# Layer 0 of a two-layer FFT convolution: the upper half of a row's base bank moves into the next row's mix

## The chip, the cores and the metric

The kernel runs on one core of one Trainium2 chip. The metric is the device time of one execution in microseconds (us). Five engines work side by side, each through its own instructions in order: TensorE (PE; its weight loads are listed apart as PEld), VectorE (DVE), ScalarE (ACT), GpSimd (POOL) and SyncE (SP, which here issues most DMAs). They meet at semaphores only.

## The reference, cut to what matters

```
# x: (8, 16, 512, 512) f32; w_real, w_imag: (16, 16, 3, 3); b_real, b_imag: (16,)
X  = rfftn(gn(x), axes=(-2, -1))                       # gn: group norm, 8 groups
Yr = conv3x3(Xr, wr) - conv3x3(Xi, wi) + b_real        # on the spectrum
Yi = conv3x3(Xr, wi) + conv3x3(Xi, wr) + b_imag
x  = x + irfftn(Yr + 1j * Yi)                          # layer 0
x  = x + mean_filter_15x15(gn(x))                      # layer 1
```

A 3x3 convolution of the spectrum is, in the image, a product with cosines and sines of the row and column number. So layer 0 needs no transform: per image row it mixes the 16 channels with a matrix that depends on the row, multiplies three such mixtures by 1, a cosine and a sine along the row, and adds them. As only half of the spectrum is convolved, each mixture takes the row itself (g) and its Hilbert transform along the row (h), a fixed 512-wide convolution.

## The kernel before, in words

The eight images run one after the other; first layer 0, then layer 1. A partition holds one channel and one block of 64 rows (16 channels x 8 blocks = 128 partitions), so a step over t = 0..63 handles eight rows of every channel at once; "a row" below is such a step. Each f32 operand is split into a high and a low f16 part, and each product is made of three f16 products.

Per row n of layer 0:

- **ACT** normalises the row (L750 into the high part of gp, L753 into g32). **POOL** subtracts for the low part (L1291, `split_g`).
- **PE** transposes it (L442, 8 matmuls, `front_turn`); **ACT** copies the transpose to SBUF (L759); **PE** does the Hilbert product (L452, 12 matmuls, `front_hilbert`) into `h_ps`; **ACT** keeps its high part (L767) and **DVE** the low part (L1096, `low_hilbert`, signal `h_split`).
- **PE** mixes (`mix`, L556 and L570). The array is used as four 64x64 tiles. "Lower" matmuls read partitions 0 to 63, "upper" ones 64 to 127; each half-term is one matmul to either half of the output. There are three PSUM banks to fill: the base p0 (in a ring of four banks), and p1 and p2, of which there is one each. Each bank takes three lower and three upper half-terms, p0 also two wrap terms. A mix has ten steps r = 0..9, each with a lower and an upper part (4 matmuls of 64x512), that write different banks. Since both parts add to the same bank at different steps, the second one waits for a semaphore of the first (`p1_half`, `p0_half`, `p2_half`).
- **DVE** multiplies p1 and p2 by the waves (L1138, L1144, `wave_terms`, signals `t1_done`, `t2_done`); **POOL** adds the two (L1298) and adds the image row (L1300, signal `q_done`); **DVE** adds p0 and writes the row (L1153) and takes its statistics (L1156): `finish_row`. Later **DVE** makes a correction per parity (L1163, `half_mean`), which **ACT** adds to the row (L775, `add_half_row`). For rows 1 to 6 and 57 to 63 **POOL** also sums rows for layer 1 (L1311, L1314, `presum`): in slots 6 to 12 and at the end.
- **SP** fetches the row's matrices from DRAM, 192 KB and 32 KB, into a ring of four (`fetch`), as soon as `p0_ready` tells that the old ones are read.

The order of all this is written out by hand. In slot n PE does `front_hilbert(n+1)`, `front_turn(n+2)`, `mix(n)`; ACT `normalise(n+3)`, `keep_hilbert(n+1)`, `keep_turned(n+2)`, `add_half_row(n-4)`; DVE `wave_terms(n-1)`, `half_mean(n-3)`, `low_hilbert(n+1)`, `finish_row(n-2)`; POOL `split_g(n+3)`, `add_terms(n-1)`. NG = 4 rows are written out and looped over (`Fori`), the first and last rows stand outside the loop. The gp buffers are a ring of NG, the hp buffers (high and low part of h) a ring of two.

## Time and profile before

| | |
|---|---|
| three runs | 4042.79 us (median), 4030.65 and 4044.06 us |
| profiled execution | 4036.1 us, its span 4034.3 us |
| granted TensorE clock, mean | 0.962 |
| busy share of PE, DVE, ACT, POOL | 90%, 81%, 59%, 65% |
| layer 0 of one image | some 305 us of a period of some 482 us |

The times are in us from the start of the span; a matmul's duration in the trace runs to the end of its drain, so consecutive matmuls overlap, and the distance of two starts is what a step costs. "Idle before" counts gaps of an engine; "issue" is a gap for which the profile shows no releaser.

### The profile page before, as it was taken

The page shows a single profiled execution, that of the slowest core. Times are in us where ns is not written, and L with a number is a line of the kernel's source. Part 1 is how long each engine was busy: PE and PEld are TensorE (multiplying, and loading weights), DVE is VectorE, ACT ScalarE, POOL GpSimd, SP SyncE. Part 2 cuts the span into 40 slices and gives each one's busy share as a digit, 9 for nine tenths or more (in the row PEclk, how much of TensorE's full clock was granted, in tenths as well). Part 3 has the DMA queues.
Part 4 walks back from the last instruction along what each step waited for, and adds up shares of the span by engine and source line. Part 5 has one row for each costly group of instructions (what it writes and reads, how often), then busy time and mean ns, then how long its engine had stood idle before and what let it go on. Part 6 is the DMA issues. An engine that isn't in the chain of part 4 may idle for free.

```text
span 4034.3 us, 124977 instructions
## 1 busy us (share of the span) xinstructions
PE 3628.3 (90%) x42592; PEld 2549.3 (63%) x42592; DVE 3254.2 (81%) x6382; ACT 2386.4 (59%) x3774; POOL 2638.4 (65%) x2177
## 2 busy tenths in 40 slices
PE   3299989998999989999899997999899998999988
PEld 1166576665766667666676666666576665766667
DVE  7878877887778878788787887788877887879986
ACT  0078733886348852588427883288733886248852
POOL 5078853887539865488546885388853986638865
PEclk8599999999999999999999999999999999999999
DMA  7511156111751118311382114711165111741114
GB/s 162 168 44 52 42 170 180 51 52 32 217 145 50 52 47 244 101 52 52 94 237 61 52 50 134 213 46 52 39 191 162 53 52 34 228 129 51 52 50 137
DMA packets 228434, 406.73 MB, mean 101 GB/s; under 512 B 98160, under 2 KB 173520, under 8 KB 215888
## 3 DMA queue, kind: packets, MB, share of 16 engines
q1 hardware_dynamic: 205776, 285.88, 24.7%
q10 hardware_dynamic: 22400, 117.46, 10.9%
q8 instruction: 156, 2.56, 0.3%
q14 instruction: 102, 0.84, 0.1%
HBM read 256.31 MB, written 146.80 MB: 100 GB/s over the span
## 4 chain that ended last, share of the span: by engine, by line
PE 70%; POOL 9%; DVE 9%; issue 7%; ACT 3%; ACTq 1%; DMA 1%; SPq 1%; POOLq 0%; DVEq 0%
PE p L556 21%; PE h_ps L651 14%; PE h_ps L452 14%; PE p L677 6%; PE xt_ps L442 5%; PE p L490 4%; POOL ob_all L1298 3%; POOL arena L1291 2%; PE h_ps L556 2%; POOL ob_all L1300 2%; PE p L570 2%; DVE ob_all L1223 2%; ACT arena L720 1%; POOL arena L1314 1%; PE p L459 1%
## 5 line engine op out<-in xcount | busy, mean ns | idle before, releaser
L556 PE MATMUL p<-arena,bd_all 64*64 64x512 f16 x16896 | 1343.7, 381 | 19.6 <-issue 11.9
L1291 POOL TENSOR_TENSOR arena<-arena 128x512 f16<-128x512 f32 x512 | 593.6, 1159 | 518.8 <-ACT arena L753 499.3
L556 PEld LDWEIGHTS p<-arena,bd_all 64*64 64x64 f16 x16896 | 606.9, 105 | 450.5 <-issue 279.3
L1349 POOL TENSOR_TENSOR arena<-img 128x512 f32<-128x512 f32 x392 | 499.2, 1274 | 468.8 <-PE h_ps L651 443.4
L720 ACT ACTIVATE arena<-h_ps 128x512 f16<-128x512 f32 x512 | 305.6, 597 | 840.9 <-PE h_ps L651 596.5
L452 PE MATMUL h_ps<-hilbert,arena 128*128 128x256 f16 x6144 | 759.6, 273 | 0.0
L452 PEld LDWEIGHTS h_ps<-hilbert,arena 128*128 128x128 f16 x6144 | 560.4, 98 | 267.4 <-issue 195.0
L1300 POOL TENSOR_TENSOR ob_all<-ob_all,img 128x512 f32<-128x512 f32 x512 | 663.5, 1296 | 79.3 <-POOL ob_all L1298 66.8
L1298 POOL TENSOR_TENSOR ob_all<-ob_all 128x512 f32<-128x512 f32 x512 | 656.9, 1283 | 31.5 <-DVE ob_all L1144 30.5
L750 ACT ACTIVATE arena<-img,sc 128x512 f16 (+1 forms) x512 | 442.1, 864 | 327.9 <-PE p L570 215.0
L1096 DVE SCALAR_TENSOR_TENSOR arena<-h_ps,arena 128x512 f16<-128x512 f32 x512 | 353.1, 690 | 268.0 <-ACT arena L767 268.0
L759 ACT ACTIVATE arena<-xt_ps 128x1024 f16<-128x1024 f16 x512 | 518.7, 1013 | 35.2 <-PE xt_ps L442 35.2
L651 PE MATMUL h_ps<-bd_all,arena 128*128 128x128 f32 x3584 | 539.5, 286 | 0.0
L775 ACT ACTIVATE img<-img,half_row (+1 forms) x1024 | 488.8, 534 | 74.4 <-DVE half_row L1163 74.4
L651 PEld LDWEIGHTS h_ps<-bd_all,arena 128*128 128x128 f32 x3584 | 447.6, 191 | 121.2 <-issue 115.1
L1207 DVE TENSOR_TENSOR arena<-h_ps,arena 128x512 f16<-128x512 f32 x512 | 353.3, 690 | 206.5 <-ACT arena L720 205.1
L1138 DVE SCALAR_TENSOR_TENSOR ob_all<-p,bias_c,cosw 128x256 f32<-128x256 f32 x1024 | 442.1, 474 | 2.4 <-issue 2.0
L1144 DVE SCALAR_TENSOR_TENSOR ob_all<-p,bias_c,cosw 128x256 f32<-128x256 f32 x1024 | 444.0, 475 | 0.0
L753 ACT ACTIVATE arena<-img,sc 128x512 f32 (+1 forms) x512 | 433.6, 847 | 4.3 <-POOL arena L1291 4.3
L1156 DVE BATCH_NORM_STATS2 stat<-img (+1 forms) x512 | 355.6, 694 | 62.8
L677 PE MATMUL p<-band,arena 128*128 128x135 f16 (+1 forms) x4096 | 332.4, 224 | 61.7 <-DVE ob_all L1223 60.3
L490 PE MATMUL p<-img,bd_all 128*64 128x256 f32 x2048 | 310.9, 411 | 72.8 <-POOL bd_all L1270 47.0
(163 smaller groups left out, 4686.4 us busy)
## 6 DMA issues: line engine op xcount, KB each, us to landing
out<-ob_all SPq DMA_DIRECT2D x512, 256.0 KB, 4.1
bd_all<-bd_dram SPq DMA_DIRECT2D x512, 192.0 KB, 2.3
img<-in_x ACTq DMA_DIRECT2D x168, 512.0 KB, 7.1
img<-in_x ACTq DMA_DIRECT2D x112, 256.0 KB, 4.8
wrap_mat<-tab_wrap_h SPq DMA_DIRECT2D x512, 32.0 KB, 2.0
img<-in_x SPq DMA_DIRECT2D x24, 512.0 KB, 24.6
bd_dram<-ob_all SPq DMA_DIRECT2D x16, 768.0 KB, 3.5
img<-in_x SPq DMA_DIRECT2D x16, 256.0 KB, 7.3
```

The costliest lines, as they stand in the source:

```text
L452: m = mm(dst(a), xT[:, 4 * lx + k, 0:rows], tb["hilbert16"][:, lt, k, 0:cols], start=(half == 0 and i == 0), stop=(half == 1 and i == 2))
L490: m = mm(uv_ps[i * HP:(i + 1) * HP, cols], w, img[:, 2 * q + i, cols], start=(q == 0 and part == 0), stop=(q == T // 2 - 1 and part == 1), ...
L556: m = mm(bank[out_half * HP:(out_half + 1) * HP, :], low(half, 6 * lm + (j if own else j + 1)), (g_part if own else h_part)(half, lp), sta ...
L651: m = mm(turned_ps[u % 2][:, k, :], row[:, k * P:(k + 1) * P], mat, start=(i == 0), stop=(i == len(terms) - 1))
L677: m = mm(p0[0][:, lo:hi], parts[u % 2][:, l, k, :], tb["band16"][:, lo - k * P + R:hi - k * P + R], start=(u == 0 and k == 0 and l == 0), ...
L759: nc.scalar.activation(xT.rearrange("p k (s m) -> p k s m", s=2)[:, :, ::-1, :], xt_ps[:].rearrange("p k (s m) -> p k s m", s=2), ACT.Iden ...
L775: ins = nc.scalar.activation(row, row, ACT.Identity, bias=half_row[:, s, a:a + 1])
L1144: ins = V.scalar_tensor_tensor(t2[:, a, :], p2[:, a * HALF:(a + 1) * HALF], bias_c[:, 0, t, 1 - a:2 - a], sinw[:, a, :], ALU.add, ALU.mult)
L1291: G.tensor_tensor(gp[s][:, 1, :], g32, gp[s][:, 0, :], ALU.subtract).then_inc(g_split, 1)
L1298: G.tensor_tensor(q, term_row[s % 2][0], term_row[s % 2][1], ALU.add).then_inc(t_added, 1)
L1300: G.tensor_tensor(q, q, parity(img[:, t, :]), ALU.add).then_inc(q_done, 1)
L1349: G.tensor_tensor(diff[u % 2], img[:, u + R, :], img[:, u - R - 1, :], ALU.subtract).then_inc(moved, 1)
```

## The change: one part of the mix is put off by a row, rings get longer, one DVE operation changes place

What it does, part by part:

- `mix(n)` opens p1 (lower) and p2 (upper) first. The lower part then does p0(n) and its lower wrap term and ends with p2; the upper part does, in steps 3, 4, 8 and 9, what is left of the *previous* row's p0 (`late_base(n-1)`: its upper half-terms and upper wrap term, signal `p0_ready` for row n-1), and p1 in steps 5 to 7. The wait for `t2_done` moves to the front of the mix. After row 63 a `late_base` of its own closes the last base bank.
- NG becomes 8 for the gp ring and for the loop bodies; a new RB = 4 is the ring of p0, of the fetched matrices and of hp (before 2). The arena grows from 12 to 16 rows of 2 KB, and the scratch that the program keeps for DMA descriptors is set to 8192 bytes.
- In a DVE slot `finish_row(n-2)` stands ahead of `low_hilbert(n+1)`.

```diff
 NU = 3 * C
 NV = P
 QUARTER = HALF // 4
-NG = 4
+NG = 8
+RB = 4
 GROUP_T = 4
 REC = 12 * HP
...
+        arena = sb("arena", [P, 16 * W])
+        piece = [arena[:, i * W:(i + 1) * W] for i in range(16)]
         g32 = piece[0]
         gp = [piece[1 + s].bitcast(F16).rearrange("p (l j) -> p l j", l=2) for s in range(NG)]
-        uv32, uvT = piece[8], piece[9].rearrange("p (k m) -> p k m", k=4)
-        xT = piece[5].bitcast(F16).rearrange("p (k m) -> p k m", k=8)
-        hp = [piece[6 + s].bitcast(F16).rearrange("p (l a n) -> p l a n", l=2, a=2) for s in range(2)]
-        smat = arena[:].bitcast(F16).rearrange("p (t j o) -> p t j o", t=T, j=12)
+        uv32, uvT = piece[7], piece[8].rearrange("p (k m) -> p k m", k=4)
+        xT = piece[9].bitcast(F16).rearrange("p (k m) -> p k m", k=8)
+        hp = [piece[10 + s].bitcast(F16).rearrange("p (l a n) -> p l a n", l=2, a=2) for s in range(RB)]
+        smat = arena[:, 0:12 * W].bitcast(F16).rearrange("p (t j o) -> p t j o", t=T, j=12)
...
@@ -376,12 +377,12 @@
                     sp.dma_start(wrap_mat[s][:], tab["wrap_h16"][t]).then_inc(bd_in[s], 16)
 
                 sp.wait_ge(uv_summed, PRIMED + (b + 1) * NCH)
-                for t in range(NG):
+                for t in range(RB):
                     fetch(t, t)
-                with sp.Fori(1, T // NG) as i:
-                    for s in range(NG):
-                        sp.wait_ge(p0_ready, b * T + i * NG + (PRIMED + s - NG + 1))
-                        fetch(i * NG + s, s)
+                with sp.Fori(1, T // RB) as i:
+                    for s in range(RB):
+                        sp.wait_ge(p0_ready, b * T + i * RB + (PRIMED + s - RB + 1))
+                        fetch(i * RB + s, s)
 
             with sp.Fori(0, B - 1) as b:
@@ -537,56 +538,53 @@
                     if first * NG + s + 2 < T:
                         front_turn(n + 2, (s + 2) % NG)
 
-                def mix(i, s, first):
-                    n = b * T + i * NG + s
-
-                    def low(h, j):
-                        return bd[s][h * HP:(h + 1) * HP, j, :]
-
-                    def g_part(h, l):
-                        return gp[s][h * HP:(h + 1) * HP, l, :]
-
-                    def h_part(h, l):
-                        return hp[s % 2][h * HP:(h + 1) * HP, l]
+                def operands(s):
 
                     def half_terms(bank, j, i3, half, opens, closes):
                         lm, lp = ((0, 0), (0, 1), (1, 0))[i3]
+                        rows = slice(half * HP, (half + 1) * HP)
                         for own in (True, False):
                             out_half = half if own else 1 - half
+                            part = gp[s][rows, lp, :] if own else hp[s % RB][rows, lp]
                             m = mm(bank[out_half * HP:(out_half + 1) * HP, :],
-                                   low(half, 6 * lm + (j if own else j + 1)),
-                                   (g_part if own else h_part)(half, lp),
+                                   bd[s % RB][rows, 6 * lm + (j if own else j + 1), :], part,
                                    start=opens and i3 == 0, stop=closes and i3 == 2, skip_group_check=True)
                         return m
-                    pe.wait_ge(bd_in[s], 32 * (b * (T // NG) + i + 1))
-                    pe.wait_ge(h_split, PRIMED + n + 1)
-                    pe.wait_ge(t1_done, PRIMED + n)
-                    if first > 0:
-                        pe.wait_ge(x1_done, PRIMED + n - (NG - 1))
-                    pe.sem_inc(mix_step, 1)
 
                     def wrap_terms(half, closes):
                         for out_half in (half, 1 - half):
-                            m = mm(p0[s][out_half * HP:(out_half + 1) * HP, :],
-                                   wrap_mat[s][half * HP:(half + 1) * HP, out_half * HP:(out_half + 1) * HP],
+                            m = mm(p0[s % RB][out_half * HP:(out_half + 1) * HP, :],
+                                   wrap_mat[s % RB][half * HP:(half + 1) * HP, out_half * HP:(out_half + 1) * HP],
                                    wrap_row[half * HP:(half + 1) * HP, :], start=False, stop=closes,
                                    skip_group_check=True)
                         return m
+                    return half_terms, wrap_terms
+
+                def late_base(s, steps):
+
+                    half_terms, wrap_terms = operands(s)
+                    for i3 in steps:
+                        if i3 < 3:
+                            half_terms(p0[s % RB], 0, i3, 1, False, False)
+                        else:
+                            wrap_terms(1, True).then_inc(p0_ready, 1)
...
+                        elif r == 6:
                             if first == 0 and s == 0:
                                 pe.wait_ge(v_wrap, b + 1)
                                 pe.sem_inc(mix_step, 1)
                             wrap_terms(0, False).then_inc(p0_half, 1)
-                        elif r < 7:
-                            if r == 4:
-                                pe.wait_ge(p1_half, n + 1)
-                                pe.sem_inc(mix_step, 1)
-                            m = half_terms(p1[:], 2, r - 4, 0, False, True)
@@ -597,27 +595,33 @@
 
                     def upper(r):
                         if r < 3:
-                            m = half_terms(p1[:], 2, r, 1, True, False)
+                            m = half_terms(p2[:], 4, r, 1, True, False)
                             if r == 2:
-                                m.then_inc(p1_half, 1)
-                        elif r < 6:
-                            if r == 3:
-                                pe.wait_ge(t2_done, PRIMED + n)
+                                m.then_inc(p2_half, 1)
+                        elif r in (3, 4, 8, 9):
+                            if first * NG + s > 0:
+                                if r == 3:
+                                    pe.wait_ge(p0_half, n)
+                                    pe.sem_inc(mix_step, 1)
+                                late_base((s - 1) % NG, (r - 3,) if r < 5 else (r - 6,))
+                        else:
+                            if r == 5:
+                                pe.wait_ge(p1_half, n + 1)
                                 pe.sem_inc(mix_step, 1)
-                            m = half_terms(p2[:], 4, r - 3, 1, True, False)
-                            if r == 5:
-                                m.then_inc(p2_half, 1)
-                        elif r < 9:
-                            if r == 6:
-                                pe.wait_ge(p0_half, n + 1)
-                                pe.sem_inc(mix_step, 1)
-                            half_terms(p0[s], 0, r - 6, 1, False, False)
-                        else:
-                            wrap_terms(1, True).then_inc(p0_ready, 1)
-
+                            m = half_terms(p1[:], 2, r - 5, 1, False, True)
+                            if r == 7:
+                                m.then_inc(p1_ready, 1)
+
+                    pe.wait_ge(bd_in[s % RB], 32 * (b * (T // RB) + i * (NG // RB) + s // RB + 1))
+                    pe.wait_ge(h_split, PRIMED + n + 1)
+                    pe.wait_ge(t1_done, PRIMED + n)
+                    pe.wait_ge(t2_done, PRIMED + n)
+                    if first * NG + s >= RB:
+                        pe.wait_ge(x1_done, PRIMED + n - (RB - 1))
+                    pe.sem_inc(mix_step, 1)
                     for r in range(10):
-                        for part in ((upper, lower) if r in (4, 7) else (lower, upper)):
-                            part(r)
+                        lower(r)
+                        upper(r)
 
                 front(0, 0, 0)
...
@@ -640,6 +644,9 @@
                 for s in range(NG):
                     front(T // NG - 1, s, T // NG - 1)
                     mix(T // NG - 1, s, T // NG - 1)
+                pe.wait_ge(p0_half, (b + 1) * T)
+                pe.sem_inc(mix_step, 1)
+                late_base(NG - 1, range(4))
                 group_mean(b * 2 + 2)
                 group_variance(b * 2 + 2)
 
@@ -762,14 +769,15 @@
 
                 def keep_hilbert(n, s, first=1):
                     act.wait_ge(h_made, PRIMED + n + 1)
-                    if first * NG + s > 1:
-                        act.wait_ge(p0_ready, PRIMED + n - 1)
-                    nc.scalar.activation(hp[s % 2][:, 0], halves(h_ps[:, 0]), ACT.Identity,
+                    if first * NG + s >= RB:
+                        act.wait_ge(p0_ready, PRIMED + n - (RB - 1))
+                    nc.scalar.activation(hp[s % RB][:, 0], halves(h_ps[:, 0]), ACT.Identity,
                                          scale=1.0 / TAB_SCALE).then_inc(h_kept, 1)
...
                     if t + 2 < T:
                         keep_turned(n + 2)
                     if t >= 4:
-                        add_half_row(n - 4, i * NG + s - 4, s)
+                        add_half_row(n - 4, i * NG + s - 4, (s - 4) % NG)
 
                 for s in range(NG):
...
@@ -1170,10 +1178,10 @@
                         wave_terms(n - 1, i * NG + s - 1, (s - 1) % NG, first - (s < 1))
                     if t >= 3:
                         half_mean(n - 3, i * NG + s - 3, (s - 3) % NG, first - (s < 3))
+                    if t >= 2:
+                        finish_row(n - 2, i * NG + s - 2, (s - 2) % NG, first - (s < 2))
                     if t + 1 < T:
                         low_hilbert(n + 1, (s + 1) % NG)
-                    if t >= 2:
-                        finish_row(n - 2, i * NG + s - 2, (s - 2) % NG, first - (s < 2))
 
                 slot(0, 0, 0)
                 virtual_means()
@@ -1374,7 +1382,7 @@
     import concourse.bacc as bacc
     from concourse.bass_utils import run_bass_kernel_spmd
 
-    nc = bacc.Bacc("TRN2", target_bir_lowering=False, num_devices=1)
+    nc = bacc.Bacc("TRN2", target_bir_lowering=False, num_devices=1, dynamic_dma_scratch_size=8192)
     arrays, args = {}, []
```

On PE, the opening of a mix in the loop. `p0_0` and `h_ps` are banks of the p0 ring. Before:

```order
L565 REGISTER_ALU [waits t1_done]
L556 MATMUL p0_0<-arena,bd_all 64x512 [waits x1_done]
L556 MATMUL p0_0<-arena,bd_all 64x512
L556 MATMUL p1<-arena,bd_all 64x512 x2
L556 MATMUL p0_0<-arena,bd_all 64x512 x2
```

With the change:

```order
L549 MATMUL p1<-arena,bd_all 64x512 [waits t2_done,x1_done,t1_done,bd_in0,h_split]
L549 MATMUL p1<-arena,bd_all 64x512
L549 MATMUL p2<-arena,bd_all 64x512 x2
L549 MATMUL p1<-arena,bd_all 64x512 x2
L549 MATMUL p2<-arena,bd_all 64x512 x2
```

The first matmul now waits for `t2_done` too, and the banks p1 and p2 are opened in place of p0 and p1.

On PE, the middle of the same mix, from step 3 on. Before:

```order
L570 MATMUL p0_0<-wrap_row,wrap_mat0 64x512 x2
L556 MATMUL p2<-arena,bd_all 64x512 [waits t2_done]
L556 MATMUL p2<-arena,bd_all 64x512 x3
L556 MATMUL p1<-arena,bd_all 64x512 [waits p1_half]
L556 MATMUL p1<-arena,bd_all 64x512 x3
L556 MATMUL p2<-arena,bd_all 64x512 x2
L556 MATMUL p1<-arena,bd_all 64x512 x2
L556 MATMUL p0_0<-arena,bd_all 64x512 [waits p0_half]
L556 MATMUL p0_0<-arena,bd_all 64x512 x3
L556 MATMUL p2<-arena,bd_all 64x512 [waits p2_half]
L556 MATMUL p2<-arena,bd_all 64x512 x3
```

With the change (`p0_2` is the bank of the row before):

```order
L549 MATMUL p0_0<-arena,bd_all 64x512 x2
L549 MATMUL p0_2<-arena,bd_all 64x512 [waits p0_half]
L549 MATMUL p0_2<-arena,bd_all 64x512
L549 MATMUL p0_0<-arena,bd_all 64x512 x2
L549 MATMUL p0_2<-arena,bd_all 64x512 x2
L549 MATMUL p0_0<-arena,bd_all 64x512 x2
L549 MATMUL p1<-arena,bd_all 64x512 [waits p1_half]
L549 MATMUL p1<-arena,bd_all 64x512
L556 MATMUL p0_0<-wrap_row,wrap_mat0 64x512 x2
L549 MATMUL p1<-arena,bd_all 64x512 x2
L549 MATMUL p2<-arena,bd_all 64x512 [waits p2_half]
L549 MATMUL p2<-arena,bd_all 64x512
```

Each bank's second half now stands three steps (p1) and five steps (p2) behind its first half's last matmul, where it stood two and two steps behind before, counted from the step of the signal to the step of the wait; `p0_half` is that of the row before.

On DVE, one slot of the loop. Before:

```order
L1163 SCALAR_TENSOR_TENSOR half_row<-stat,known 128x2
L1095 REGISTER_ALU
L1096 SCALAR_TENSOR_TENSOR arena<-h_ps,arena 128x512 [waits h_kept]
L1153 ISA [waits p0_ready,q_done]
L1153 SCALAR_TENSOR_TENSOR img<-p0_2,sc,ob_all 128x2x256
L1156 ISA [waits x1_done]
L1156 BN_STATS stat<-img 128x6
```

With the change:

```order
L1171 SCALAR_TENSOR_TENSOR half_row<-stat,known 128x2
L1161 ISA [waits p0_ready,q_done]
L1161 SCALAR_TENSOR_TENSOR img<-p0_1,sc,ob_all 128x2x256
L1164 ISA [waits x1_done]
L1164 BN_STATS stat<-img 128x6
L1103 REGISTER_ALU
L1104 SCALAR_TENSOR_TENSOR arena<-h_ps,arena 128x512 [waits h_kept]
```

The two operations of `finish_row` have passed the low half of h.

## Rows read from the trace of the kernel before

**Rows 1.** The page's head: span, then busy time and share of each engine.
```profile
span 4034.3 us, 124977 instructions
...
PE 3628.3 (90%) x42592; PEld 2549.3 (63%) x42592; DVE 3254.2 (81%) x6382; ACT 2386.4 (59%) x3774; POOL 2638.4 (65%) x2177
```
**Rows 2.** Busy time in 20 rows' stretch of layer 0: PE, PEld, DVE, ACT, POOL, clock.
```profile
314.00:402.40 88.40, 88.40 (x1202) 57.17 (x1201) 73.88 (x161) 77.22 (x121) 73.98 (x61) 1.00 0.19 52
```
**Rows 3.** Who waited for whom in that stretch: us, times, longest.
```profile
DVE arena L1096 <- ACT arena L767: 11.7, 20, 0.6
POOL arena L1291 <- ACT arena L753: 10.6, 20, 0.6
PEld p L556 <- issue: 10.1, 40, 0.3
ACT arena L750 <- PE p L570: 8.4, 15, 0.6
...
ACT arena L750 <- PE h_ps L570: 3.4, 6, 0.6
```
**Rows 4.** Timeline, one row on PE and PEld: start, us, what, count [idle before].
```profile
350.14 0.84 PE L556 MATMUL p<-arena,bd_all 64*64 64x512 f16 x12
350.59 0.11 PEld L570 LDWEIGHTS p<-wrap_row,wrap_mat 64*64 64x64 f16 x2
350.81 0.38 PE L570 MATMUL p<-wrap_row,wrap_mat 64*64 64x512 f16 x2
351.11 0.46 PEld L556 LDWEIGHTS p<-arena,bd_all 64*64 64x64 f16 x12 [0.18 <-issue]
351.14 0.80 PE L556 MATMUL p<-arena,bd_all 64*64 64x512 f16 x9
351.90 0.17 PEld L556 LDWEIGHTS p<-arena,bd_all 64*64 64x64 f16 x6 [0.32 <-issue]
352.36 0.41 PE L556 MATMUL p<-arena,bd_all 64*64 64x512 f16 x2
352.69 1.48 PE L452 MATMUL h_ps<-hilbert,arena 128*128 128x256 f16 x12
354.01 0.61 PE L442 MATMUL xt_ps<-ident,arena 128*128 128x128 f16 x8
354.56 0.84 PE L556 MATMUL p<-arena,bd_all 64*64 64x512 f16 x12
```
**Rows 5.** Timeline, the other engines over the same row.
```profile
352.83 0.86 DVE L1138 SCALAR_TENSOR_TENSOR ob_all<-p,bias_c,cosw 128x256 f32<-128x256 f32 x2
353.61 0.86 DVE L1144 SCALAR_TENSOR_TENSOR ob_all<-p,bias_c,cosw 128x256 f32<-128x256 f32 x2
354.39 0.15 DVE L1163 SCALAR_TENSOR_TENSOR half_row<-stat,known 128x2 f32 x1
354.54 0.57 ACT L767 ACTIVATE arena<-h_ps 128x512 f16<-128x512 f32 x1
355.15 0.69 DVE L1096 SCALAR_TENSOR_TENSOR arena<-h_ps,arena 128x512 f16<-128x512 f32 x1 [0.61 <-ACT arena L767]
355.76 0.74 DVE L1153 SCALAR_TENSOR_TENSOR img<-h_ps,sc,ob_all 128x512 f32 x1
356.64 0.69 DVE L1156 BATCH_NORM_STATS2 stat<-img  x1
```
**Rows 6.** Timeline of POOL, first and last of seven presums, and rows between.
```profile
246.26 1.28 POOL L1311 TENSOR_TENSOR arena<-img 128x512 f32<-128x512 f32 x1
...
267.36 1.15 POOL L1291 TENSOR_TENSOR arena<-arena 128x512 f16<-128x512 f32 x1
272.30 1.16 POOL L1291 TENSOR_TENSOR arena<-arena 128x512 f16<-128x512 f32 x1
276.03 1.28 POOL L1314 TENSOR_TENSOR arena<-arena,img 128x512 f32<-128x512 f32 x1
```
**Rows 7.** Timeline of PE there: the Hilbert products of following rows.
```profile
262.61 1.48 PE L452 MATMUL h_ps<-hilbert,arena 128*128 128x256 f16 x12
267.02 1.48 PE L452 MATMUL h_ps<-hilbert,arena 128*128 128x256 f16 x12
271.73 1.48 PE L452 MATMUL h_ps<-hilbert,arena 128*128 128x256 f16 x12
276.66 1.48 PE L452 MATMUL h_ps<-hilbert,arena 128*128 128x256 f16 x12
281.62 1.49 PE L452 MATMUL h_ps<-hilbert,arena 128*128 128x256 f16 x12
286.41 1.48 PE L452 MATMUL h_ps<-hilbert,arena 128*128 128x256 f16 x12
```
**Rows 8.** The chain at the end of an image: ACT's branch to the next image.
```profile
1152.39 4.36 issue
1156.75 0.06 ACTq L877
```
**Rows 9.** The page's DMA issues of the fetched matrices: KB, us to landing.
```profile
bd_all<-bd_dram SPq DMA_DIRECT2D x512, 192.0 KB, 2.3
...
wrap_mat<-tab_wrap_h SPq DMA_DIRECT2D x512, 32.0 KB, 2.0
```

**Rows 10.** Timeline at the end of an image's layer 0: last mix, last row.
```profile
497.12 0.41 PE L556 MATMUL p<-arena,bd_all 64*64 64x512 f16 x2
...
502.14 0.75 DVE L1153 SCALAR_TENSOR_TENSOR img<-p,sc,ob_all 128x512 f32<-128x512 f32 x1 [1.22 <-POOL ob_all L1300]
```

35 lines of the change are left out of this document (19 added, 16 removed).

## The prediction, made before the kernel was run

> **What bounds the kernel now.** I read the page's head first [rows 1]: PE is busy 90% of the span, DVE 81%. Such shares are an average over two layers, so next came the table of stretches for 20 rows in the middle of layer 0 [rows 2]. There PE is busy for all of 88.40 us, at a granted clock of 1.00, which is the higher of its two levels (2.4 GHz); a row costs 88.4 / 20 = 4.42 us. DVE is busy 73.88 / 20 = 3.69 us a row, ACT 77.22 / 20 = 3.86, POOL 73.98 / 20 = 3.70. The waits of that stretch [rows 3] say the same from the other side: DVE, ACT and POOL each stand idle some 0.5 to 0.6 us per row, and PE's matmuls never do. So PE sets the row, and a wait of the other three is worth nothing by itself. But "busy" counts a matmul to the end of its drain, and hides what PE loses between starts. What gives it away is the line of PEld: 40 gaps in 20 rows, 10.1 us in all, two a row, before weights of the mix.
>
> The timeline of one row shows them [rows 4]. The mix opens at 350.14, step 2 starts at 350.59, step 3 at 350.81: the first step costs 0.24 us, each further one 0.215. At that pace step 4 would follow at 351.025; but the lower part, which waits for p1_half there, starts at 351.14: 0.115 lost. Three steps on, step 7 should start at 351.785; its weights, held by p2_half, come at 351.90, and a matmul starts 0.03 after its weights (as 351.11 and 351.14): 351.93, so 0.145 lost. From there to the last step is 2 x 0.215 again (352.36). Sum 0.26 us a row; both are the time that a signal takes from a matmul's start to the start of the one that waits: 350.59 to 351.14 is 0.55, and for p2_half 351.355 to 351.93 is 0.57. The mix takes 2.55, the Hilbert product 1.32, the transposes 0.55.
>
> **The change part by part.**
>
> *The order of the mix.* Matmuls and weight loads stay the same in number. p1_half now has three steps between signal and wait, 0.645 against the 0.55 to 0.57 needed; p2_half five; p0_half is a row old. Both stalls go, with 0.08 to spare for the tighter one. As the two parts no longer run apart (0.03 at the end of the mix) I take 0.27 a row: 4.42 becomes 4.15. Bounds: one of the two signals still late would leave 0.12 of it; more than 0.30 isn't there to be gained, as ten steps, the Hilbert product and the transposes stay.
>
> *The wait for t2_done in front of the mix.* Behind it stand all matmuls of the mix, and behind these all of DVE's next row. In the trace t2 of the row before ends at 353.61 + 0.86 = 354.47 and the mix opens at 354.56 [rows 4, 5]: with DVE's old phase this wait would decide at once. But that phase is late without need: DVE idles 0.61 before L1096 [rows 3, 5], where it waits for ACT, and the row's end stands behind it. In the new order the end of the row comes first and fills that hole. p1 is complete with step 7, whose matmuls start 0.24 + 6 x 0.215 = 1.53 after the opening; with 0.55 for the signal DVE can start L1138 at 2.08; L1138 and L1144 take 354.47 - 352.83 = 1.64, so t2 is done at 3.72, and a signal of at most 0.2 later is 3.92, under 4.15. DVE's own round is 4.42 - 0.61 = 3.81 and fits as well. Cost nothing, with 0.2 to 0.3 of cover.
>
> *Low half of h behind the row's end.* It ends a round of 3.81 after L1138's start, 5.89 after the opening. The Hilbert product that needs it starts one row and one mix later, 4.15 + (2.55 - 0.27) = 6.43. Cost nothing, 0.5 of cover. This cover is gone where POOL delays the end of a row, as DVE then stands before L1153 with the low half behind it.
>
> *Rings.* The gp ring of eight takes away ACT's wait for the mix (L750, 8.4 + 3.4 = 11.8 us of 20 rows [rows 3]), hp's ring of four one that isn't seen. ACT isn't the bound: worth nothing, bounds 0 and 0.1 a row. p0_ready comes a row later, so SP fetches a row later: it has two rows, 8.3 us, where 2.3 and 2.0 us are needed [rows 9]. Nothing.
>
> *The presums.* Here it costs. With a presum POOL needs 272.30 - 267.36 = 4.94 a row [rows 6], seven rows long (246.26 to 276.03). Before, POOL falls behind by 7 x (4.94 - 4.42) = 3.6 us, of which PE lost: its rows last 4.71, 4.93, 4.96 and 4.79 in place of 4.42 [rows 7], 1.7 us. With rows of 4.15 POOL falls behind by 7 x 0.79 = 5.5. Before, 1.9 were absorbed; now the way over the row's end and the low half has only the 0.5 found above, so I take 5.0 (bounds 3.6 and 5.5). That is 3.3 more than before (1.9 to 3.8).
>
> *Start and end of an image.* After row 63 PE has four steps more, some 0.9 us. PE's last matmul starts at 497.12, the last row is finished at 502.14, held by POOL [rows 10]: hidden. The first two rows wait for other things; 0, between -0.5 and +0.5.
>
> *Sum.* 60 of the 63 rows behind the first have a Hilbert product ahead and gain: 60 x 0.27 = 16.2. Less 3.3: 12.9 us an image, 103 for eight. Layer 1 keeps its instructions. The profiled execution took 4036.1 us (span 4034.3), so 3933. The three runs' mean is 3 us above the profiled one, their median 7; I give 3936.
>
> **The rivals.**
>
> *A wait on another engine eats part of it.* Covers of 0.08 (p1_half), 0.2 (t2_done) and 0.3 (ACT's 3.86 against 4.15, DVE's 3.81) are thin, and all of them are sized at the old phases. For it: three engines come within 0.3 of PE. Against it: none of their rounds exceeds 4.15. If half a stall (0.13) comes back, 60 x 8 x 0.13 = 62 us: 3998.
>
> *It gains more.* If POOL's delay in the presums is absorbed as before, and the mixes lose their last 0.03: 4036 - 8 x (60 x 0.30 - 1.9) = 3907.
>
> *The stalls only change place.* If t2_done keeps the phase of the trace, the opening comes at 354.47 + 0.14 = 354.61, later than now, and the round through DVE and the mix would hold at about 4.42: 4036, no change. Against it: the 0.61 of idle time in front of L1096 is there to be used.
>
> *The longer loop bodies miss their instructions: slower.* The inner loops now have 8 rows written out in place of 4. In the trace a jump back costs nothing there: the rows from 262.61 to 267.02, or from 350.14 to 354.56, are all 4.42. But at the jump to the next image, over a long body, ACT stands for 4.36 us [rows 8]. If a body of 8 rows is too long for an engine's store of instructions, each of 5 jumps in 8 images costs that: 40 x 4.36 = 174, less 103 gained: 4107. It decides from 103 / 40 = 2.6 us a jump on. The Trainium skill ("Runtime: NRT & Kernel Launch", Instruction fetch mechanics) says that a taken branch to a page outside the window forces a fetch before execution goes on; 4.36 us of standing at the long jump agree. It gives PE 128 KiB and the others 32, and in the same section a window of two lines of 16 KiB. PE runs 120 matmuls and loads a row [rows 2]; at the page's 64 bytes each, eight rows are an estimated 61 KB, inside the first figure and outside the second, as four rows (31 KB) barely are inside. ACT, DVE and POOL, with 6, 8 and 3 operations a row [rows 2], have bodies far shorter than that. By the second figure PE would jump to a page that is gone, by the first not.
>
> **How the numbers follow.** The forecast 0.62, with a range of its own from 3918 to 3958 (0.03 a row is 14 us, the presums' bounds 11 and 4, the start 4, the runs' spread 7). Part eaten 0.16, more gained 0.07, stalls moved 0.06, slower 0.09. A measurement of this kernel tells 0.3% (12 us) from no change; so faster 0.85, same 0.06, slower 0.09. The range for 8 in 10 takes in the forecast and most of the part-eaten case: 3905 to 3995.
>
> **What would show it.** Right: rows of 4.15 us in the middle of layer 0 with PE still busy throughout and no PEld gap of 0.18 and 0.32 inside the mix; L1104 (low half) behind L1164 with no idle time before it; ACT's wait for L556 (the wrap matmul) gone; five or six rows of 4.94 around the presums in each image, with PE's wait on DVE or POOL there. Wrong: a gap before each mix's first weights released by L1152 (t2_done); rows of 4.3; a stall of some us once in eight rows on PE (the jump); or a period of alternating rows, which would mean a ring of waits through two engines that this sum treats one by one.

## The result, and the profile after

The changed kernel took 4029.48 us (median of 20 runs, 4024.04 to 4033.87) against 4037.36 (20 runs, 4029.03 to 4044.44) for the kernel before: ratio 0.9978, 95% interval 0.9972 to 0.9984. That is 8 us, inside the 0.3% called no change, where 3936 was forecast.

In the tables below a row of layer 0 is the time from one row's Hilbert product to the next, and "an image's rows" is the time from its first to its last, read at the first image: 280.5 us before, 280.4 after. The other images lie within 0.5 us of the first, but for the last one of the profile before, which took 284.6. So the rows did not change in sum, though they were to lose 12.9 us.

The page's head after, the span, the busy time of each engine and what the final chain ran over:
```profile
span 4028.9 us, 122552 instructions
...
PE 3515.2 (87%) x42592; PEld 2538.7 (63%) x42592; DVE 3445.0 (86%) x6382; ACT 2382.8 (59%) x3774; POOL 2638.3 (65%) x2177
...
PE h_ps L658 14%; PE p L549 11%; PE h_ps L453 9%; PE p L684 6%; PE p L491 4%; POOL ob_all L1306 3%; DVE arena L1104 3%; DVE ob_all L1152 3%; DVE half_row L1171 3%; PE xt_ps L443 3%; DVE img L1161 2%; POOL ob_all L1308 2%; POOL arena L1299 2%; DVE ob_all L1231 2%; ACT arena L727 1%
```
The same stretch as in [rows 2], after (PE, PEld, DVE, ACT, POOL, clock), and the waits in it, which answer to [rows 3]:
```profile
314.00:402.40 88.40, 83.83 (x1204) 56.95 (x1200) 85.55 (x161) 76.65 (x121) 73.66 (x61) 1.00 0.19 51
```
```profile
PEld h_ps L453 <- issue: 12.3, 17, 0.9
ACT arena L774 <- PE h_ps L453: 12.1, 21, 0.8
POOL arena L1299 <- ACT arena L760: 11.7, 21, 0.8
PE h_ps L453 <- DVE arena L1104: 4.3, 10, 0.5
```
Read these against [rows 1 to 3]. PE is no longer busy throughout: 4.6 of 88.4 us are idle, and it stands in front of the Hilbert product for DVE's low half, in one row of two. ACT's wait for the wrap matmul and PEld's 40 gaps inside the mix are gone, as the change intends. DVE has the same 161 instructions in the stretch as before but 85.55 us of work in place of 73.88: 11.7 us, 0.58 a row, that no instruction was added for. The page says 3445.0 for 3254.2 over the whole span. A count that stays and a busy time that grows is the line to stop at: some instruction takes longer.

It is the half mean, a SCALAR_TENSOR_TENSOR on two elements a partition. Below, an instruction is said to stand while it is on its engine, counted as busy, and does not finish because another engine's instruction has not. DVE's timeline over two rows after (answers to [rows 5]):
```profile
353.35 0.64 DVE L1171 SCALAR_TENSOR_TENSOR half_row<-stat,known 128x2 f32 x1
353.91 0.74 DVE L1161 SCALAR_TENSOR_TENSOR img<-h_ps,sc,ob_all 128x512 f32 x1
354.79 0.69 DVE L1164 BATCH_NORM_STATS2 stat<-img  x1
355.40 0.67 DVE L1104 SCALAR_TENSOR_TENSOR arena<-h_ps,arena 128x512 f16<-128x512 f32 x1
356.04 0.88 DVE L1146 SCALAR_TENSOR_TENSOR ob_all<-p,bias_c,cosw 128x256 f32<-128x256 f32 x2
356.83 0.87 DVE L1152 SCALAR_TENSOR_TENSOR ob_all<-p,bias_c,cosw 128x256 f32<-128x256 f32 x2
357.62 0.99 DVE L1171 SCALAR_TENSOR_TENSOR half_row<-stat,known 128x2 f32 x1
...
360.03 0.67 DVE L1104 SCALAR_TENSOR_TENSOR arena<-h_ps,arena 128x512 f16<-128x512 f32 x1
```
and POOL's over the same time:
```profile
352.81 1.16 POOL L1299 TENSOR_TENSOR arena<-arena 128x512 f16<-128x512 f32 x1 [0.34 <-ACT arena L760]
...
357.44 1.16 POOL L1299 TENSOR_TENSOR arena<-arena 128x512 f16<-128x512 f32 x1 [0.74 <-ACT arena L760]
...
361.65 1.16 POOL L1299 TENSOR_TENSOR arena<-arena 128x512 f16<-128x512 f32 x1 [0.34 <-ACT arena L760]
```
The half mean took 0.15 in [rows 5]; here 0.64 and 0.99. It ends at 353.99 and 358.61; POOL's low part of g ends at 353.97 and 358.60. The longer it takes, the earlier it began in POOL's instruction; the end is always POOL's end. Over the whole span it took 144.2 us before (median 151 ns, 116 of 512 over 250 ns) and 360.7 after (median 690, 416 over 250, longest 1220), and each long one ends 14 to 16 ns (median; at most 21) after a tensor_tensor of POOL. The converse holds too: of the 512 half means, those that began outside a POOL instruction, or with less than 0.15 us of it left, all took at most 168 ns (386 before, 90 after). Of two that begin together the half mean can be the one that goes first: in five rows after, the half mean began at most 0.04 us behind the start of POOL's low part of g and took 0.15, and POOL's instruction took 1.19 to 1.22 in place of 1.16 (the first at 236.25). Of the other lines of DVE's row none got longer. In the row of [rows 5] it began at 354.39, between one POOL instruction that ended at 354.19 and the next that began at 354.71.

The hint was in the profile of before. The table of groups, with forms kept apart, has (busy, mean ns):
```profile
L1163 DVE SCALAR_TENSOR_TENSOR half_row<-stat,known 128x2 f32 x416 | 106.4, 256 | 0.0
L1163 DVE SCALAR_TENSOR_TENSOR half_row<-stat,known 128x2 f32<-128x2 f32 x96 | 37.2, 394 | 0.0
```
A mean of 256 and 394 ns for an instruction whose row in the timeline reads 0.15 says that it has two durations. It also sets right what stands ahead of the prediction, that the engines "meet at semaphores only": here two of them meet in an instruction that waits for no semaphore.

**Why just 4.42 us again.** After the presums the rows alternate, 4.13 to 4.29 and 4.58 to 4.73, mean 4.42. The same rows close a ring over two rows. The half mean ends with POOL's instruction at 353.97; the row's end, the statistics and the low half follow, to 356.07 (2.10); PE's Hilbert product starts at 356.14 (0.07); then PE and ACT:
```profile
356.14 1.48 PE L453 MATMUL h_ps<-hilbert,arena 128*128 128x256 f16 x12
```
```profile
357.74 0.60 ACT L774 ACTIVATE arena<-h_ps 128x512 f16<-128x512 f32 x1 [0.38 <-PE h_ps L453]
358.23 1.02 ACT L766 ACTIVATE arena<-xt_ps 128x1024 f16<-128x1024 f16 x1
359.14 0.95 ACT L783 ACTIVATE img<-img,half_row  x2
359.99 0.84 ACT L757 ACTIVATE arena<-img,sc 128x512 f16 x1
360.72 0.86 ACT L760 ACTIVATE arena<-img,sc 128x512 f32 x1
```
ACT's high half starts 1.60 after the Hilbert product, its queue is through with g at 361.58 (3.84), POOL's low part of g starts at 361.65 and ends at 362.81 (1.23), and the half mean of that row, begun at 362.19, ends at 362.83. 2.10 + 0.07 + 1.60 + 3.84 + 1.23 = 8.84 us for two rows, 4.42 each. The other row of the pair has a ring of its own (358.60 to 367.44, again 8.84). The old bound was PE's 4.42, the new one a ring through DVE, PE, ACT and POOL that has the same length by chance: the experiments below move the one without the other.

### The profile page after: what moved, and what is told of

The parts are those of the page before. It is cut to its first block, busy times and chain, and to the rows that moved or that the text cites. A ratio compares the mean times of both kernels' runs of the same rounds, so it can differ in the third digit from the quotient of the medians.

```text
span 4028.9 us, 122552 instructions
## 1 busy us (share of the span) xinstructions
PE 3515.2 (87%) x42592; PEld 2538.7 (63%) x42592; DVE 3445.0 (86%) x6382; ACT 2382.8 (59%) x3774; POOL 2638.3 (65%) x2177
## 3 DMA queue, kind: packets, MB, share of 16 engines
q14 instruction: 150, 1.23, 0.1%
## 4 chain that ended last, share of the span: by engine, by line
PE 52%; DVE 21%; issue 11%; POOL 8%; ACT 5%; ACTq 1%; DVEq 1%; SPq 1%; DMA 0%; POOLq 0%
PE h_ps L658 14%; PE p L549 11%; PE h_ps L453 9%; PE p L684 6%; PE p L491 4%; POOL ob_all L1306 3%; DVE arena L1104 3%; DVE ob_all L1152 3%; DVE half_row L1171 3%; PE xt_ps L443 3%; DVE img L1161 2%; POOL ob_all L1308 2%; POOL arena L1299 2%; DVE ob_all L1231 2%; ACT arena L727 1%
## 5 line engine op out<-in xcount | busy, mean ns | idle before, releaser
L549 PE MATMUL p<-arena,bd_all 64*64 64x512 f16 x16896 | 1206.4, 379 | 30.0 <-DVE ob_all L1152 29.6
L727 ACT ACTIVATE arena<-h_ps 128x512 f16<-128x512 f32 x512 | 305.7, 597 | 841.4 <-PE h_ps L658 593.9
L774 ACT ACTIVATE arena<-h_ps 128x512 f16<-128x512 f32 x512 | 305.0, 596 | 319.7 <-PE h_ps L453 319.5
L1146 DVE SCALAR_TENSOR_TENSOR ob_all<-p,bias_c,cosw 128x256 f32<-128x256 f32 x1024 | 445.6, 477 | 33.8 <-PE p L549 29.6
L1152 DVE SCALAR_TENSOR_TENSOR ob_all<-p,bias_c,cosw 128x256 f32<-128x256 f32 x1024 | 443.5, 475 | 0.0
```

The costliest lines, as they stand in the source:

```text
L549: m = mm(bank[out_half * HP:(out_half + 1) * HP, :], bd[s % RB][rows, 6 * lm + (j if own else j + 1), :], part, start=opens and i3 == 0, s ...
L1152: ins = V.scalar_tensor_tensor(t2[:, a, :], p2[:, a * HALF:(a + 1) * HALF], bias_c[:, 0, t, 1 - a:2 - a], sinw[:, a, :], ALU.add, ALU.mult)
```

## The experiments

| run | mix, rings | DVE order | half mean | median us | ratio (interval) | an image's rows | half mean, sum |
|---|---|---|---|---|---|---|---|
| before | old, 4 | old | two sources | 4037 | 1 | 280.5 | 144 |
| after | new, 8 | new | two sources | 4029.5 | 0.9978 | 280.4 | 361 |
| e1 | new, 8 | new | one source | 3939.6 | 0.9751 (0.9737 to 0.9764) | 269.7 | 209 |
| e2 | old, 4 | old | one source | 4030.6 | 0.9975 (0.9966 to 0.9985) | 280.5 | 209 |
| e3 | new, 8 | old | two sources | 3999.7 | 0.9901 (0.9885 to 0.9916) | 275.6 | 330 |
| e4 | old, 8 | old | two sources | 4015.4 | 0.9936 (0.9921 to 0.9951) | 279.0 | 357 |
| e5 | new, 8 | old | one source | 3977.3 | 0.9849 (0.9833 to 0.9865) | 274.3 | 209 |
| e6 | old, 8 | old | one source | 4014.1 | 0.9935 (0.9922 to 0.9949) | 279.0 | 209 |
| e7 | new, 8 | new | two sources | 3990.4 | 0.9879 (0.9864 to 0.9894) | 275.4 | 228 |
| e8 | new, 8 | new | one source | 3917.0 | 0.9696 (0.9683 to 0.9709) | 266.8 | 209 |
| e9 | new, 8 | new | one source | 3899.8 | 0.9659 (0.9646 to 0.9673) | 265.2 | 211 |
| e10 | old, 8 | old | two sources | 4032.6 | 0.9990 (0.9981 to 0.9998) | 280.4 | 118 |
| e11 | old, 4 | new | two sources | 4039.2 | 1.0004 (0.9995 to 1.0014) | 282.0 | 245 |

Each ratio is to the kernel before on the same chip; that one's median was 4040.7 beside e1 to e4, 4039.1 beside e5 to e8 and 4036.3 beside e9 to e11, so medians of different groups can be compared to some 4 us only. One source has two operations of 0.20 us a row, hence the larger floor of 209 us.

**e1, the half mean without a second tensor.**
```
-V.scalar_tensor_tensor(half_row[:, s, :], stat[:, t, 1:6:3], -0.5, known[:, t, :],
-                       ALU.mult, ALU.add).then_inc(half_made, 1)
+for a in range(2):
+    ins = V.tensor_scalar(half_row[:, s, a:a + 1], stat[:, t, 1 + 3 * a:2 + 3 * a], -0.5,
+                          known[:, t, a:a + 1], ALU.mult, ALU.add)
+ins.then_inc(half_made, 1)
```


> The changed kernel, with the half mean of a row (L1171, one scalar_tensor_tensor over two tensors in SBUF, 128x2) made by two tensor_scalar operations that read one tensor each and take the known mean as a per-partition scalar. Theory (the half mean stands until POOL's running operation ends, since it reads two SBUF tensors): no half mean over 0.3 us, DVE busy under 80 of 88.4 us in the middle of layer 0, rows of 4.15 to 4.2 us there and 4.95 around the presums, time 3925 to 3955 us. Rival (the changed order or the longer ring delays DVE by itself, and the half mean only shows it): rows stay at 4.42 on average, 4025 to 4035 us. Second rival (an operation with one SBUF source also takes the shared way): each of the two stands, time 4030 to 4100 us.


3939.6 us: 90 us from one edit that adds 512 instructions. DVE's busy time, 80.99, is 1 over the 80 expected. DVE, then POOL, over the same stretch of time as above:
```profile
352.46 0.32 DVE L1172 TENSOR_SCALAR half_row<-stat,known 128x1 f32 x2
352.70 0.74 DVE L1161 SCALAR_TENSOR_TENSOR img<-p,sc,ob_all 128x512 f32 x1
...
356.57 0.32 DVE L1172 TENSOR_SCALAR half_row<-stat,known 128x1 f32 x2
```
```profile
352.23 1.16 POOL L1301 TENSOR_TENSOR arena<-arena 128x512 f16<-128x512 f32 x1 [0.32 <-ACT arena L760]
...
356.52 1.16 POOL L1301 TENSOR_TENSOR arena<-arena 128x512 f16<-128x512 f32 x1 [0.39 <-ACT arena L760]
```
It falls inside the same POOL instruction and is done in 0.32 for both halves (203 ns median, none of 1024 over 250). The stretch of 20 rows, with PE busy again throughout:
```profile
314.00:402.40 88.40, 88.35 (x1265) 62.92 (x1263) 80.99 (x191) 81.07 (x127) 77.57 (x64) 1.00 0.21 55
```
Rows are 4.14 to 4.25, and in each image the end of the layer is 1.5 us shorter (16.6 to 15.1 from the last Hilbert product to the next statistics), as the half means there no longer stand.

**e2, the same edit on the kernel before.**


> The kernel before, with the same two tensor_scalar operations in place of its L1163. Theory: it loses the 67 us of DVE time that L1163 stands over 0.15 us in all, but these lie at the ends of images and around the presums, so the time falls by 0 to 15 us only, rows stay at 4.42, set by PE. Rival (DVE was near the bound before too): rows get shorter than 4.42 and the time falls by over 20 us.


4030.6 us, rows 280.5 as before, image ends 1.4 us shorter, which is all of the 10 us gained. So the edit is worth 90 us with the change and 10 without it: it is not a gain of its own that would hide a change worth nothing.

**e3, the changed kernel with DVE's old order.**
```
+if t + 1 < T:
+    low_hilbert(n + 1, (s + 1) % NG)
 if t >= 2:
     finish_row(n - 2, i * NG + s - 2, (s - 2) % NG, first - (s < 2))
-if t + 1 < T:
-    low_hilbert(n + 1, (s + 1) % NG)
```


> The changed kernel with DVE's old order (the low half of h ahead of the end of a row), half mean as changed. Theory (the half mean's stand is set by POOL's operations alone): it stands here too, DVE is the bound, rows of 4.3 to 4.5 us, 4010 to 4060 us. Rival (the new DVE order is what costs): rows fall to 4.15 to 4.24 and the time to 3930 to 3970 us.


3999.7 us, between the two ranges: 10 under the theory's, 30 over the rival's. Taken alone this would say that the new order costs 30 us. It does not hold once the stand is gone: e5.

**e4, the rings alone** (old mix and order, eight and four buffers).


> The kernel before with the rings alone (gp ring and loop bodies of eight, p0, matrices and hp rings of four), old mix, old DVE order. Theory: PE keeps rows of 4.42, as its own work is the same; but ACT no longer waits for the mix, so POOL's split of g starts earlier and lies over the half mean, which then takes 0.3 us or more in most rows, hidden in DVE's 0.6 us of idle time; 4030 to 4045 us. Rival (longer bodies cost at the jumps): 4050 us or more.


4015.4 us, 15 under the range expected, though the half mean takes 357 us here too. The rows are 4.42 all the same: PE sets them with its stalls, and DVE had 0.6 a row to stand in. DVE and POOL in the stretch, the end of the one again the end of the other (356.74, 356.73):
```profile
356.14 0.60 DVE L1165 SCALAR_TENSOR_TENSOR half_row<-stat,known 128x2 f32 x1
```
```profile
355.57 1.16 POOL L1293 TENSOR_TENSOR arena<-arena 128x512 f16<-128x512 f32 x1 [0.55 <-ACT arena L754]
```
What the rings give is in the presums, two rows of 4.78 and 4.68 in place of four from 4.71 to 4.96 [rows 7], 1.1 us an image, and in the fourth row (5.13 to 4.64).

**e5, one source and the old order** (the edits of e1 and e3 together).


> The changed kernel with two edits of DVE's work: the half mean as two one-source operations, which did not stand against GpSimd in the first experiment (203 ns, none over 250), and the old order (low half in front of the row's end). If the half mean's stand is all that kept the rows long, the order hardly matters once it is gone: 3940 to 3955 us, rows of 4.15 to 4.25 us. Rival: the old order costs by itself (the low half, 1.16 us, made in front of the half mean's row end, holds the row's answer back, and the 30 us by which the run with the old order beat the change came from the half mean alone falling elsewhere): then about 3975 us and rows of 4.28 us or more. Under the second rival, that the old order is better in itself, it would be faster than 3935 us.


3977.3 us: the rival. (The low half takes 0.67 us, not the 1.16 given there.) With the half mean out of the way the new order is worth 38 us (3939.6), with it standing it costs 30 (4029.5 to 3999.7). The order decides also where the half mean falls: with the old order its stand costs 22 us (3999.7 to 3977.3), with the new one 90. With the old order the low half waits for ACT; of the waits of e5's stretch:
```profile
DVE arena L1104 <- ACT arena L774: 5.3, 18, 0.4
```
So the row's end and the next row's products with the waves come later, and PE waits for them (t2_done). In this stretch the Hilbert product takes 1.32 and the mix 2.29 in every row, from start to start; only the time from the transposes to the mix varies, 0.54 to 0.93, where it was 0.54 before, and the mix opens 0.34 to 0.40 after the end of L1152 each time.

**e6, rings and one source.**


> Old mix and old DVE order, rings of eight and four only, with the one-source half mean. In the run of the rings alone the half mean stood 356 us in sum, mostly in DVE's idle time, with rows of 4.42 us set by the matrix engine and its two signal stalls. If that reading holds, taking the stand away gives little: the ends of the images (1.5 us each, 12 us in all), so 4002 to 4008 us, rows still 4.42 us. Rival: the stand is on the rows' path here too; then rows of about 4.3 us and 3950 to 3970 us.


4014.1 us, 6 over the range, rows 279.0 as in e4: the theory on the rows held to the tenth. The images' ends are shorter in the trace (16.56 to 15.2 each, some 10 us in all), but the median fell by 1: between these ends and the next image's first row, where no edit reaches, e6's profiled run took 1306.5 us for 1299.8 in e4. That stretch varies by some 4 us from image to image in every run.

**e7, GpSimd's low part of g in quarters.** DVE's instructions are those of the changed kernel.
```
-G.tensor_tensor(gp[s][:, 1, :], g32, gp[s][:, 0, :], ALU.subtract).then_inc(g_split, 1)
+for k in range(4):
+    q = slice(k * W // 4, (k + 1) * W // 4)
+    ins = G.tensor_tensor(gp[s][:, 1, q], g32[:, q], gp[s][:, 0, q], ALU.subtract)
+ins.then_inc(g_split, 1)
```


> The changed kernel with GpSimd's low part of g (128x512, 1.16 us) issued as four instructions of 128 columns; DVE and the matrix engine untouched. If the half mean stands until the GpSimd instruction that runs beside it ends, it now stands at most about 0.35 us where it met this one: its sum falls from 361 us to 180 to 230 us, rows go from 4.42 to 4.15 to 4.3 us, the whole to 3945 to 3985 us, in spite of three more instructions on GpSimd in each row (some 0.1 us each by a guess). Rival: what is slow is the half mean itself or DVE's new order, not the lock against one instruction: then the sum stays near 361 us and the time at 4029 us or above, since GpSimd has more to do.


3990.4 us, 5 over the expected range, with more work on POOL and 39 us less in all; the half mean's sum, 228, is inside its range. Rows behind the presums are 4.13 to 4.43. The half mean goes on standing, but now against the sum in front of the quarters (ends 353.82 and 353.80):
```profile
353.35 0.47 DVE L1171 SCALAR_TENSOR_TENSOR half_row<-stat,known 128x2 f32 x1
```
```profile
352.51 1.29 POOL L1311 TENSOR_TENSOR ob_all<-ob_all,img 128x512 f32<-128x512 f32 x1 [0.19 <-POOL ob_all L1309]
353.76 1.59 POOL L1301 TENSOR_TENSOR arena<-arena 128x128 f16<-128x128 f32 x4
```
The quarters take 1.59 for 1.16, 0.14 for each further instruction, so rows with a presum are 5.38 and not 4.95. That is what was left out of the expectation: 6 x 0.43 x 8 = 21 us.

**e8 and e9, presums spread.** On top of e1, POOL adds one row in every three of its slots, where it added one in each of eight in a run:
```
-for t in range(R + 9):
-    slot(t // NG, t % NG, t // NG, sum_t=t - 5 if 5 <= t <= R + 5 else None)
+for t in range(32):
+    slot(t // NG, t % NG, t // NG, sum_t=t // 3 - 1 if t % 3 == 0 and 3 <= t <= 24 else None)   # e8
+    slot(t // NG, t % NG, t // NG, sum_t=t // 3 - 2 if t % 3 == 0 and 6 <= t <= 27 else None)   # e9
```


> The changed kernel with the one-source half mean and the presums of the first rows spread, one in three rows (after rows 3, 6, ... 24) and not eight in a run. In the first experiment the presum rows took 4.76 to 4.81 and five times 4.95 us beside 4.20, about 5 us per image over the others, since GpSimd's row is 4.95 us with a presum. GpSimd has 4.95 + 2 x 3.7 = 12.4 us in three rows, the matrix engine 12.6, and the ring of eight gives it three rows of room. Theory: the loss goes, 4.6 us x 8 = 37 us off 3939.6, so 3900 to 3906 us. Rival: GpSimd's lateness reaches the row it happens in (the answer of the row before it waits for its sum), so that spreading only moves the loss: 3935 to 3945 us.


3917.0 us: 11 over the range, because one row took 5.90. The wait in it, of the stretch from 240 to 256:
```profile
PE h_ps L453 <- DVE arena L1104: 1.6, 1, 1.6
```


> As the run with the presums spread one in three rows, but each three rows later (after rows 6, 9, ... 27). There the first presum fell on a row in which GpSimd was still behind from the start of the image (it had stood on ScalarE's rows 2 and 3), and one row took 5.90 us where its neighbours took 4.15. Theory: GpSimd makes up 4.15 - 3.7 = 0.4 us a row without a presum, so by row 9 it is level, the long row goes, and 1.75 us x 8 = 14 us come off 3917: 3901 to 3906 us. Rival: the first presum is late for another reason (it waits for ScalarE's add to its own row), and the long row only moves: 3914 to 3920 us.


3899.8 us, 1 under the range: the long row is gone and came back nowhere. Hilbert products on PE, first of e1, where each waits, then of e9 over nearly the same time:
```profile
264.79 1.47 PE L453 MATMUL h_ps<-hilbert,arena 128*128 128x256 f16 x12 [0.75 <-DVE arena L1104]
269.74 1.47 PE L453 MATMUL h_ps<-hilbert,arena 128*128 128x256 f16 x12 [0.76 <-DVE arena L1104]
274.70 1.47 PE L453 MATMUL h_ps<-hilbert,arena 128*128 128x256 f16 x12 [0.76 <-DVE arena L1104]
```
```profile
263.33 1.48 PE L453 MATMUL h_ps<-hilbert,arena 128*128 128x256 f16 x12
267.48 1.49 PE L453 MATMUL h_ps<-hilbert,arena 128*128 128x256 f16 x12
271.62 1.48 PE L453 MATMUL h_ps<-hilbert,arena 128*128 128x256 f16 x12
```
e9 is the fastest kernel of the study, 3.4% under the kernel before.

**e10, the rings with ACT's old wait.**
```
-act.wait_ge(p0_ready, PRIMED + n - (NG - 1))
+act.wait_ge(p0_ready, PRIMED + n - (RB - 1))
```


> The rings alone (old mix, old DVE order), and ScalarE waits again for the base bank of the row four before (row n - 3's count), as in the kernel before, although the ring of eight would let it go on. Theory: it is the removal of this wait that moved GpSimd's low part of g onto the half mean; put back, the half mean falls in GpSimd's gap again, its sum goes from 356 us to about 144 us (between 130 and 180), and the time goes from 4015 us back to 4030 to 4042 us, because GpSimd's start is tied again in the rows with presums. Rival: the moved buffers or the base ring of ScalarE's other product are behind the shift, and the sum stays at 340 to 360 us and the time near 4015 us.


4032.6 us and 118 us of half mean, less than the 130 I had as the lowest: one wait of ACT, which bounds no row in the middle of the layer, decides whether DVE's instruction stands. DVE and POOL, the half mean at 353.76 to 353.91, in POOL's gap from 353.56 to 354.08:
```profile
353.76 0.15 DVE L1165 SCALAR_TENSOR_TENSOR half_row<-stat,known 128x2 f32 x1
```
```profile
352.26 1.30 POOL L1302 TENSOR_TENSOR ob_all<-ob_all,img 128x512 f32<-128x512 f32 x1 [0.19 <-POOL ob_all L1300]
354.08 1.16 POOL L1293 TENSOR_TENSOR arena<-arena 128x512 f16<-128x512 f32 x1 [0.52 <-ACT arena L754]
```

**e11, DVE's new order alone** (the order of e3's diff the other way, on the kernel before).


> The kernel before with DVE's new order alone (the end of the old row in front of the low half of the next). With the half mean as two one-source operations the new order was worth 38 us beside the new mix; here the old mix holds the row at 4.42 us, and the matrix engine's wait for the low half had 0.5 us of cover, so 4034 to 4043 us with the same rows. Rival: the order costs by itself because the low half comes later than the matrix engine wants it: rows over 4.45 us and a time above 4055 us.


4039.2 us, no difference. Rows are 4.41 to 4.42 in the middle; the presums last six rows of 4.87 to 5.07 and cost 1.5 us an image more. The half mean takes 245 us in all, hidden, and stands against POOL's last sum (DVE 355.16, POOL 355.15):
```profile
354.79 0.37 DVE L1163 SCALAR_TENSOR_TENSOR half_row<-stat,known 128x2 f32 x1
```
```profile
353.85 1.30 POOL L1300 TENSOR_TENSOR ob_all<-ob_all,img 128x512 f32<-128x512 f32 x1 [0.19 <-POOL ob_all L1298]
```

## Why the prediction was wrong

**The step that failed** is the sentence "DVE's own round is 4.42 - 0.61 = 3.81 and fits as well", with the cost nothing that the two steps on t2_done and the low half drew from it. It took the half mean at the 0.15 of one row and carried it into a new phase. Its mean after is 0.70 (360.7 / 512), DVE's rounds (from one L1146 to the next) 4.27 and 4.58, and with POOL's end as their beat the ring of 8.84. With one-source half means the round is 3.81 - 0.15 + 0.32 = 3.98 and fits in 4.15, which e1 shows.

**A second one, of the same paragraph,** cost less: "Cost nothing, with 0.2 to 0.3 of cover" for the wait for t2_done in front of the mix. The sum there was 2.08 + 1.64 + 0.2 = 3.92 from one opening of the mix to the next. In e1 the three terms are 2.19, 1.66 and 0.36, in all 4.21:
```profile
360.01 0.87 DVE L1152 SCALAR_TENSOR_TENSOR ob_all<-p,bias_c,cosw 128x256 f32<-128x256 f32 x2
...
363.43 0.88 DVE L1146 SCALAR_TENSOR_TENSOR ob_all<-p,bias_c,cosw 128x256 f32<-128x256 f32 x2 [0.22 <-PE p L549]
364.22 0.86 DVE L1152 SCALAR_TENSOR_TENSOR ob_all<-p,bias_c,cosw 128x256 f32<-128x256 f32 x2
```
```profile
361.24 1.05 PE L549 MATMUL p<-arena,bd_all 64*64 64x512 f16 x14
...
365.44 0.84 PE L549 MATMUL p<-arena,bd_all 64*64 64x512 f16 x12
```
The mix opens at 361.24 and at 365.44, each time 0.36 after L1152 (ends 360.88 and 365.08). Most of what was missing is in the last term: no row of the sum showed the 0.2, and in the stretch from 314 to 402.4 it is 0.35 to 0.40. So PE and DVE wait for each other in turn, and the row is 4.20 in place of 4.15. In the fourth row of each image, where DVE comes late, the same wait is open to see, in the changed kernel as in e1 (waits from 205 to 240):
```profile
PE p L549 <- DVE ob_all L1152: 1.6, 1, 1.6
```
This row took 5.82 us, against 5.12 before and 4.64 with the rings alone. These are readings of traces; no run has the wait at another place.

**What held, shown by e1.** The mix: 2.29 against 2.56 us, no gap inside it, rows of 4.14 to 4.25 where 4.15 was forecast, more often 4.20 for the wait just told. The presums: five or six rows of 4.95 forecast with 5.0 lost; e1 has one of 4.8 and five of 4.95 to 4.97, 4.6 lost. In sum 280.5 - 269.7 = 10.8 us an image against 12.9; of the 2.1 that is missing, the wait for t2_done took 2.3 in the 46 rows from the eighteenth on and the fourth row 1.0, and other rows gave back a part. With the 1.5 at the image's end, which I had at 0, it is 98 us in all against 103. So 3936 was the time of a kernel in which the half mean does not stand, and that kernel takes 3939.6. That the two are so close is in part luck: the 1.5 us come from the new half mean and not from the change (e2 has 1.4 of them), and with one-source half means on both sides the change is worth 91 us (e2 to e1).

**The rings, priced at nothing, were worth 22 us alone** (e4), and moved the half mean. "ACT isn't the bound: worth nothing" priced a removed wait by its own engine. Removing it let POOL's low part of g start when ACT has its input and so moved it over the half mean (e4 and e10: 357 and 118 us of half mean, with and without the wait's removal). The same removal saves 1.4 us an image in the presums and the fourth row (e10 to e4), which the step missed also. That is 11 of the 17 us between those two medians; where the others lie was not found.

**The new order of DVE: right in itself (38 us, e5 against e1), a cost with the stand (30 us, e3), nothing without the new mix (e11).** Its effect could not be added to that of the others.

**The rivals.** "A wait on another engine eats part of it" was the nearest by its kind, at 0.13 a row where 0.27 was eaten. "The stalls only change place" gave the time, 4036, but its mechanism is not what held the changed kernel: PE's waits for t2_done are three an image there (the fourth row and the last two mixes), 29.6 us in all. It is there with DVE's old order, for which it was reckoned: e5's rows are 4.30 on average, where it gave 4.42. What speaks against it in the prediction, that the idle time before the low half can be used, is what the new order then did. The longer loop bodies cost nothing: in e1 all rows from the eighteenth on, jumps among them, are 4.14 to 4.25. The last sentence of the prediction named the sign that appeared, alternating rows as a ring of waits through two engines. It was listed and not priced; that the ring would need a link that is no wait at all in the program I did not see.

The Trainium skill ("SBUF — State Buffer", Who interferes with whom) states the rule: a VectorE instruction with two SBUF inputs contends with a GpSimd instruction that reads SBUF; the ports that the two share are an exclusive lock, and the order of issue decides who blocks. The half mean is the only VectorE instruction of the row with two tensors in SBUF; the others take one of theirs from PSUM, and none of them got longer. The traces agree: over the seven runs with the old half mean every one over 250 ns ends within 25 ns of the end of a tensor_tensor of GpSimd. A rule that speaks of what overlaps has to be asked again whenever a change moves one of the two.

**Left open:** what the rings give beyond the rows; whether e6's missing 9 us are anything but the spread of the stretch between images; why e10's half mean is 118 and not 144; the cause of e8's late first presum beyond POOL's lateness, though e9 shows that placing it three rows on removes it.

## What to carry to other kernels

Before a change of phase, list the instructions that have two durations (a group's mean far from its row in the timeline), find the engine that they stand against, and price the change with the long one; such a coupling appears in no list of waits, only as busy time that grows at a constant count. A tiny instruction of two SBUF tensors on DVE beside a busy GpSimd is worth rewriting with one tensor even at twice the count. And edits that share a ring are tested as pairs: the new order was worth +30, 0 or -38 us, depending on what stood beside it.

## What the runs showed of the hardware

- A SCALAR_TENSOR_TENSOR of 128x2 with two SBUF tensors takes 0.15 us alone and up to 1.26 (e3) when it comes second beside a TENSOR_TENSOR of GpSimd, ending 14 to 19 ns after it (medians of seven runs, at most 25); GpSimd's instruction keeps its 1.16 then. Where GpSimd's had begun at most 0.04 us ahead, the small one took its 0.15 and GpSimd's 1.19 to 1.22 (five rows of the changed kernel).
- A TENSOR_SCALAR of 128x1 with its second value as a per-partition scalar from SBUF takes 0.20 and did not stand in any of some 6000 cases.
- Cutting GpSimd's 128x512 operation (1.16 us) in four costs 0.14 us per further instruction.
- Loop bodies of eight rows (120 matmuls and loads a row on PE) showed no stall at the jump back: all rows of e1 from the eighteenth on are 4.14 to 4.25.
- From the end of DVE's L1152 to the first matmul that waits for its signal it took 0.34 to 0.40 us behind the transposes (e1 and e5, 314 to 402.4) and 0.25 where PE had been idle for 1.6 us.
